# A one-core gated attention and expert block: causal mask as rows of the product, feed-forward in pairs, weights spread by a product

## What is computed

```python
xn = layernorm(x)
q, k, v = heads(xn @ Wq + bq), heads(xn @ Wk + bk), heads(xn @ Wv + bv)      # 16 heads of 8
y = softmax(where(causal, q @ k.T * D**-0.5, -inf)) @ v
y = y + softmax(qc @ kc.T * D**-0.5) @ vc     # qc = xn @ Wcq + bcq; kc, vc from the context
x = x + tanh(g_xattn) * (y @ Wp + bp)
xf = layernorm(x)
s = sigmoid(xf @ router.T); choice = s + router_bias           # 16 experts in 4 groups
# a group scores the sum of its best two choices; two groups stay; of their experts the best four
w = s[top4] / (sum(s[top4]) + 1e-20) * 2.5
x = x + tanh(g_ffn) * sum_e w[e] * (silu(xf @ wg[e].T) * (xf @ wu[e].T)) @ wd[e].T   # all 16 experts, width 64
```

## Time and profile before

| What | Value |
|---|---|
| median of 3 runs | 371.53 us (369.07 to 372.36) |
| profiled execution | 370.12 us |
| its span | 368.4 us |
| PE, DVE busy | 337.1 us (91%), 262.3 us (71%) |
| ACT, POOL busy | 199.4 us (54%), 199.3 us (54%) |
| DMA | 39.10 MB, mean 106 GB/s |

### The profile page before, as it was taken

How to read it: one execution, slowest core, us unless ns; L and a number is a source line. 1 busy time by engine, 2 the same in 40 slices (tenths; PEclk the granted TensorE clock), 3 DMA queues, 4 the chain that set the end, 5 groups by cost and what they waited for, 6 DMA issues and landing times.

```text
span 368.4 us, 8693 instructions
## 1 busy us (share of the span) xinstructions
PE 337.1 (91%) x3128; PEld 244.1 (66%) x3136; DVE 262.3 (71%) x710; ACT 199.4 (54%) x426; POOL 199.3 (54%) x296
## 2 busy tenths in 40 slices
PE   1778989999999999999999999999999999998665
PEld 0443554766776788777877877676877787766544
DVE  2228588567888878978787888777888856667752
ACT  2321256678757756665656646674666468633020
POOL 4945036608831796368824885449602842945305
PEclk9999999999999999999999999999999999999899
DMA  3254345664214653538143823183335003214060
GB/s 95 75 176 137 118 141 162 178 216 132 72 61 124 165 149 85 145 95 196 45 134 95 192 72 110 47 185 117 88 100 118 3 16 75 45 46 86 3 128 14
DMA packets 31322, 39.10 MB, mean 106 GB/s; under 512 B 2832, under 2 KB 28592, under 8 KB 28848
## 3 DMA queue, kind: packets, MB, share of 16 engines
q1 hardware_dynamic: 31280, 38.55, 38.7%
HBM read 30.89 MB, written 7.47 MB: 104 GB/s over the span
## 4 chain that ended last, share of the span: by engine, by line
PE 81%; DVE 7%; DMA 4%; ACT 3%; issue 2%; SPq 1%; POOL 1%; ACTq 0%; POOLq 0%
PE bank L743 14%; PE bank L721 13%; PE bank L708 9%; PE bank L812 7%; PE bank L813 6%; PE bank L821 6%; PE bank L705 5%; DMA k_stack<-part_scr 3%; PE bank L699 3%; PE bank L763 3%; PE bank L750 2%; PE bank L765 2%; PE bank L772 2%; PE bank L782 2%; PE bank L770 1%
## 5 line engine op out<-in xcount | busy, mean ns | idle before, releaser
L866 DVE TENSOR_REDUCE row_max<-bank 128x2 f32<-128x512 f32 (+1 forms) x224 | 149.2, 687 | 47.2 <-PE bank L708 25.7
L632 ACT ACTIVATE probs<-bank 128x512 f32<-128x512 f32 x224 | 127.9, 594 | 62.2 <-PE bank L721 49.0
L721 PE MATMUL bank<-q_stack,k_stack 73*128 73x256 bf16 (+1 forms) x512 | 80.9, 259 | 0.4 <-ACT probs L632 0.3
L547 POOL TENSOR_SCALAR_AFFINE_SELECT probs<-probs 128x256 f32<-128x256 f32 (+1 forms) x96 | 45.2, 483 | 40.1 <-ACT probs L632 39.2
L743 PE MATMUL bank<-probs,v_ext 128*32 128x256 f32 (+1 forms) x1024 | 61.1, 358 | 0.0
L560 POOL TENSOR_TENSOR f_h<-f_h,comb 128x256 f32<-128x256 f32 x64 | 45.3, 725 | 24.9 <-DMA comb<-c_scr 20.7
L708 PE MATMUL bank<-k_stack,q_stack 72*128 72x256 bf16 x256 | 50.7, 290 | 3.3 <-DMA k_stack<-part_scr 2.0
L721 PEld LDWEIGHTS bank<-q_stack,k_stack 73*128 73x128 bf16 x512 | 42.1, 98 | 16.8 <-issue 5.7
L812 PE MATMUL bank<-xn2T,w_pairs_sb 128*128 128x256 f32 x128 | 41.1, 403 | 3.4 <-DVE f_h L951 3.3
L743 PEld LDWEIGHTS bank<-probs,v_ext 128*32 128x32 f32 x1024 | 27.0, 109 | 22.5 <-issue 7.9
L944 DVE SCALAR_TENSOR_TENSOR f_gate<-f_tanh,bank 128x256 f32<-128x256 f32 x64 | 26.5, 413 | 19.9 <-ACT f_tanh L647 19.9
(11 more groups left out here) (103 smaller groups left out, 393.6 us busy)
## 6 DMA issues: line engine op xcount, KB each, us to landing
q_stack<-part_scr SPq DMA_DIRECT2D x48, 192.0 KB
k_stack<-part_scr SPq DMA_DIRECT2D x48, 192.0 KB
comb<-c_scr SPq DMA_DIRECT2D x16, 512.0 KB, 6.4
part_scr<-part SPq DMA_DIRECT2D x48, 128.0 KB, 2.0
x_in<-in_x SPq DMA_DIRECT2D x8, 128.0 KB, 2.9
w_pairs_sb<-in_w_pairs SPq DMA_DIRECT2D x1, 1024.0 KB, 7.7
out<-y_out SPq DMA_DIRECT2D x8, 128.0 KB, 1.9
ctx_in<-in_ctxT SPq DMA_DIRECT2D x8, 64.0 KB, 3.4
```

Of the source, the lines that this page charges most:

```text
L547: nc.gpsimd.affine_select(out=p, in_=p, compare_op=ALU.is_ge, fill=0.0, base=0, pattern=[[0, nh], [1, 128]], channel_multiplier=-1).then_i ...
L632: nc.scalar.activation(probs[:, seq % NP, :], exp_bank[s % 2][:, :], ACT.Exp).then_inc(exp_done, 1)
L721: last = pe.matmul(ps[:, n, :], k_stack[0:STACK + 1, b % SLOTS, kind, h, kt * 128:(kt + 1) * 128], q_stack[0:STACK + 1, b % SLOTS, kind, h ...
L866: nc.vector.tensor_reduce(row_max[:, kind, qt, h0:h0 + nh], max_bank[k % 2][:, :].rearrange("p (h k) -> p h k", h=nh), AX.X, ALU.max).then ...
```

## The change

**Causal rows.** The stacks of kind SELF get 48 more rows, 73 to 120. Of 128 tokens three share a row. A key has a factor in its own row only; a query has a large negative factor in the rows of all later keys and zero in those of earlier ones, and the three columns of a row are told apart by powers of two. The product over rows 0 to 120 is the masked score, in both passes, for the chunks' diagonal blocks; other blocks contract 72 or 73 rows as before. So a product of 256 queries over the diagonal becomes two of 128. The mask product and POOL's selections go. The rows are made once by POOL, placed in slot 0 by two DMAs and copied to slots 1 and 2 (`tri:0`, `tri:0:1`, `tri:0:2`); since row 72 lies among the rows now contracted in the first pass, a DMA zeroes it in `q_stack` with each load of a SELF stack.

**First cross stack in halves.** For sample 0 the cross stacks are loaded in halves of eight heads (`kh:0`, `qh:0`, `kh:0:1`, `qh:0:1`), all cross chunks are ordered by half, and the first shift is made and written for eight heads (`shift:0`), then for the rest (`shift:0:2`). Sample 0 is normalised on DVE (`xnv`), and so is the second layernorm of sample 7 (`xnv2`).

**Paired feed-forward.** Gates of two blocks fill one bank (`ga`), ups another (`up`); tanh, swish, the up product and POOL's product work on 512 columns, four of each a sample in place of eight. Each has one bank: the next `ga` waits for swish, the next `up` for the up product, the first `ga` of a sample for the `out` of the one before.

**Last weights by a product.** For sample 7 a 16 x 1024 matrix of ones and zeros, made by POOL in the unused tile `rest`, spreads the transposed weights over the partitions by products into four banks that the scores no longer need; ACT copies them to `comb`.

```diff
+ROW_TOKENS = 3
+ROWS = 48
+MASKED = STACK + 1 + ROWS
+AT = (2.0 ** 40, 2.0 ** -12, 2.0 ** -64)
+FROM = (2.0 ** -70, 2.0 ** -18, 2.0 ** 34)
+LATER = 2.0 ** 92
...
-S1_CHUNKS = [(CROSS, qt, 2 * g, 2, 256) for qt in range(NQ) for g in range(8)]
+S1_CHUNKS = [(CROSS, qt, H // 2 * half + 2 * g, 2, 256) for half in range(2) for qt in range(NQ) for g in range(4)]
...
-GU_USES = NB + 1
-ROUTE_STEPS = 18
+STACK_DMAS = (2 * PARTS, 2 * PARTS + 1)
+GP = NB // 2
+ROUTE_STEPS = 16
+ROUTE_WORDS = (0, 3, 6, 9, 12, 14, 16)
...
-        ident_b = sb("ident_b", [128, 128], BF16)
-        causal = sb("causal", [128, 4, 128], BF16)
+        tri_q, tri_k = (sb(n, [ROWS, 128 + ROWS * ROW_TOKENS], BF16) for n in ("tri_q", "tri_k"))
+        zero_row = sb("zero_row", [H, T], BF16)
...
+        expert_of = rest[0:E].rearrange("e k x -> e (k x)")
...
+            def place_masks(s):
+                if s == 0:
+                    sp.wait_ge(const_made, 3)
+                else:
+                    sp.wait_ge(tri_in[0], 32)
+                for st, tri in ((q_stack, tri_q), (k_stack, tri_k)):
+                    first = tri[:, 0:T].unsqueeze(1).broadcast_to([ROWS, H, T])
+                    src = first if s == 0 else st[SHIFT_ROW + 1:MASKED, 0, SELF]
+                    sp.dma_start(st[SHIFT_ROW + 1:MASKED, s, SELF], src).then_inc(tri_in[s], 16)
...
+                if kind == SELF and qk == 0:
+                    if b == 0:
+                        sp.wait_ge(const_step, 4)
+                    sp.dma_start(q_stack[SHIFT_ROW:SHIFT_ROW + 1, b % SLOTS, SELF], zero_row[:, :]).then_inc(stack_in[b % SLOTS][SELF], 16)
+            def load_first(qk, half):
+                sp.wait_ge(part_out[CROSS], 48)
+                heads = slice(half * H // 2, (half + 1) * H // 2)
+                for i in range(PARTS):
+                    src = scr[0, CROSS, qk, :, :, heads].rearrange("j d h x -> d j (h x)")
+                    if qk == 0:
+                        src = src[:, i].unsqueeze(1).broadcast_to([D, PARTS, H // 2 * T])
+                    sp.dma_start((q_stack, k_stack)[qk][i * BLOCK:(i + 1) * BLOCK, 0, CROSS, heads], src).then_inc(stack_in[0][CROSS] if half else first_heads_in, 16)
...
+                    heads = slice(H // 2 * (n // 2), H // 2 * (n // 2 + 1))
+                    sp.dma_start(q_stack[SHIFT_ROW:SHIFT_ROW + 1, 0, CROSS, heads], shiftT[heads, CROSS, :]).then_inc(shift_in[0][CROSS] if n else first_shift_in, 16)
...
+                at_q, at_k = (a[:, 128:].rearrange("p (r c) -> p r c", c=ROW_TOKENS) for a in (tri_q, tri_k))
+                for c in range(ROW_TOKENS):
+                    nc.gpsimd.memset(at_q[:, :, c:c + 1], -AT[c]).then_inc(const_step, 1)
+                    nc.gpsimd.memset(at_k[:, :, c:c + 1], FROM[c]).then_inc(const_step, 1)
+                pool.wait_ge(const_step, 4 + 2 * ROW_TOKENS)
+                earlier = dict(pattern=[[1, ROWS], [0, ROW_TOKENS]], channel_multiplier=-1)
+                nc.gpsimd.affine_select(out=at_k, in_=at_k, compare_op=ALU.is_equal, fill=0.0, base=0, **earlier).then_inc(tri_step, 1)
+                nc.gpsimd.affine_select(out=at_q, in_=at_q, compare_op=ALU.is_ge, fill=-LATER, base=0, **earlier).then_inc(tri_step, 1)
+                pool.wait_ge(tri_step, 2)
+                nc.gpsimd.affine_select(out=at_q, in_=at_q, compare_op=ALU.is_ge, fill=0.0, base=0,
+                                        pattern=[[-1, ROWS], [0, ROW_TOKENS]], channel_multiplier=1).then_inc(tri_step, 1)
+                pool.wait_ge(tri_step, 3)
+                for tri in (tri_q, tri_k):
+                    nc.gpsimd.tensor_copy(tri[:, 0:128], tri[:, 128:256]).then_inc(const_made, 1)
...
+            def mark_experts():
+                for kind in (CROSS, SELF):
+                    pool.wait_ge(split[kind], B * PARTS)
+                at = expert_of.rearrange("e (f u) -> e f u", u=I)
+                nc.gpsimd.memset(at, 1.0).then_inc(expert_step, 1)
+                pool.wait_ge(expert_step, 1)
+                nc.gpsimd.affine_select(out=at, in_=at, compare_op=ALU.is_equal, fill=0.0, base=0,
+                                        pattern=[[1, E], [0, I]], channel_multiplier=-1).then_inc(expert_step, 1)
             def combine(b, j):
-                pool.wait_ge(gu_free, b * GU_USES + j + 1)
-                if j == 0:
+                pool.wait_ge(ups_free, b * GP + j + 1)
+                if b == B - 1:
+                    pool.wait_ge(spread_done, j + 1)
+                elif j == 0:
                     pool.wait_ge(comb_in, b * 32 + 32)
-                at = f_h[:, j, :]
-                nc.gpsimd.tensor_tensor(at, at, comb[:, j, :], ALU.mult).then_inc(f_hc_done, 1)
+                at = f_h[:, 2 * j:2 * j + 2, :]
+                nc.gpsimd.tensor_tensor(at, at, comb[:, 2 * j:2 * j + 2, :], ALU.mult).then_inc(f_hc_done, 1)
...
+            def spread_out(b, j):
+                act.wait_ge(spread_ready, j + 1)
+                if j == 0:
+                    ge(act, f_hc_done, GP * b)
+                nc.scalar.activation(comb[:, 2 * j:2 * j + 2, :], spread_bank[j][:, :].rearrange("p (n x) -> p n x", n=2),
+                                     ACT.Copy).then_inc(spread_done, 1)
...
-                    pe.matmul(ps[:, :, keys - 128:keys], ident_b[:, :], causal[:, 0:nh, :], start=True, stop=False)
                 for n in range(nh):
-                    h = h0 + n
-                    q = q_stack[0:STACK, s, kind, h, qt * 128:(qt + 1) * 128]
+                    q, key = q_stack[:, s, kind, h0 + n, qt * 128:(qt + 1) * 128], k_stack[:, s, kind, h0 + n, :]
                     if kind == SELF:
-                        for kt in range(keys // 128):
-                            last = pe.matmul(ps[:, n, kt * 128:(kt + 1) * 128], q, k_stack[0:STACK, s, kind, h, kt * 128:(kt + 1) * 128],
-                                             start=False, stop=n == nh - 1 and kt == keys // 128 - 1)
+                        for kt in range(qt + 1):
+                            rows_used = MASKED if kt == qt else STACK
+                            last = pe.matmul(ps[:, n, kt * 128:(kt + 1) * 128], q[0:rows_used], key[0:rows_used, kt * 128:(kt + 1) * 128],
+                                             start=n == 0 and kt == 0, stop=n == nh - 1 and kt == qt)
...
+                    key, q = k_stack[:, b % SLOTS, kind, h, kt * 128:(kt + 1) * 128], q_stack[:, b % SLOTS, kind, h, :]
+                    if kind == SELF:
+                        for qt in range(kt, NQ):
+                            rows_used = MASKED if kt == qt else STACK + 1
+                            last = pe.matmul(ps[:, n, qt * 128 - q0:(qt + 1) * 128 - q0], key[0:rows_used], q[0:rows_used, qt * 128:(qt + 1) * 128],
+                                             start=n == 0 and qt == kt, stop=n == nh - 1 and qt == NQ - 1)
+                    else:
+                        last = pe.matmul(ps[:, n, :], key[0:STACK + 1], q[0:STACK + 1], start=n == 0, stop=n == nh - 1)
...
+            def hidden(b, j, bank_of, w):
+                for n in range(2):
+                    e0 = (2 * j + n) * 128
+                    last = pe.matmul(bank_of[:, n * T:(n + 1) * T], w[:, e0:e0 + 128], xn2T[:, :], start=True, stop=True)
+                return last
+            def gates_of(b, j):
                 if j == 0:
                     misc_evacuated(pe, "xn2T", b)
                     if b == 0:
                         pe.wait_ge(w_experts, 32)
-                use = b * GU_USES + j
-                ge(pe, gu_free, use - 1)
-                e0 = slice(j * 128, (j + 1) * 128)
-                pe.matmul(gu_bank[use % 2][:, 0:T], w_gate[:, e0], xn2T[:, :], start=True, stop=True)
-                pe.matmul(gu_bank[use % 2][:, T:2 * T], w_up[:, e0], xn2T[:, :], start=True, stop=True).then_inc(gu_ready, 1)
+                    ge(pe, out_made, b)
+                ge(pe, f_gate_done, b * GP + j)
+                hidden(b, j, gate_bank, w_gate).then_inc(gates_ready, 1)
+            def ups_of(b, j):
+                ge(pe, ups_free, b * GP + j)
+                hidden(b, j, up_bank, w_up).then_inc(ups_ready, 1)
...
+            def spread_weights(b, j):
+                if j == 0:
+                    misc_evacuated(pe, "combT", b)
+                    pe.wait_ge(expert_step, 2)
+                    pe.wait_ge(max_taken, B * NC1)
+                    pe.wait_ge(exp_done, B * NC2)
+                for n in range(2):
+                    last = pe.matmul(spread_bank[j][:, n * T:(n + 1) * T], expert_of[:, (2 * j + n) * 128:(2 * j + n + 1) * 128], combT[:, :],
+                                     start=True, stop=True)
+                last.then_inc(spread_ready, 1)
...
+                    last = nc.vector.scalar_tensor_tensor(out=r_score[:, :, :], in0=r_tanh[:, :, :], scalar=0.5,
+                                                          in1=spread(r_half[:, :].broadcast_to([128, NQ]), E), op0=ALU.mult, op1=ALU.add)
...
```

(17 more changed lines are left out.)

484 lines of the change are left out of this document (246 added, 238 removed).

## The result

| | before | after |
|---|---|---|
| median, beside each other | 370.32 us (4 runs) | 365.61 us (4 runs, 363.39 to 367.45) |
| profiled execution, span | 370.12, 368.4 | 365.4, 363.7 |

The ratio is 0.9864, 95% interval [0.9824, 0.9904]: faster by 1.4%, where 6.5% was forecast. 365.4 lies 19.0 us above the 346.4 of the sum. Stages are compared within traces; there is one trace for each kernel.

The account below looks back on a forecast made before the run. It took chains and DVE to pace the start, PE the long middle, one chain the end. 370.12 - 12.3 - 1.0 - 1.8 + 1.0 - 8.0 - 1.6 = 346.4, forecast 346 us (341 to 349, chance 0.62).

Parts of the forecast that it names:

- Mask products: PE-bound middle: removing 12 mask products a sample saves 1.76 us in each of seven samples, 12.3 us.
- rival A: Middle: hand-overs with a late DVE turn mask time into waiting, taking 9 of the 12.3 us, so 355; chance 0.12.
- Normalising on DVE: Start: normalising sample 0 on DVE instead of POOL makes all that hangs on it 1.0 us earlier.
- First exponential: Start: sample 0's first exponent product comes 2.8 us earlier, two thirds of it recovered idle time, 1.8 us.
- Single gate banks: Feed-forward: with one bank each, PE's gates wait for tanh and swish at times; charged 1.0 us.
- Routing: Sample 7's routing: two steps fewer and less slowing by POOL's products, less 0.4 given back; 1.6 us saved.
- the slow rows agree: Routing: slow steps fit the skill's two-input rule, by which rewriting frees nothing; the sum would be 1.6 us higher.
- End after routing: From sample 7's routing to the output sum: 18.1 us becomes 10.1, a gain of 8.0 us.
- Rival B: Mask-row copies delay the start up to 6 us, or sample 6's weights stall the end; 350 to 352, chance 0.14.

Follow-up runs that it names:

- m2: Kernel before with the causal rows alone, mask copies of slot 1 issued at `load:3`; 369.73 us, ratio 0.9933.
- e1: Changed kernel with POOL's memset of v_ext moved behind the second rstd; 363.2 us, ratio 0.9782.
- e3: e1 with the start's loads and stores in order of need and slot 1's mask copies issued at `load:3`; 364.66 us, ratio 0.9832.
- c1: m2 with eight unread products in sample 0 where mask products stood; 367.88 us, ratio 0.9942.
- m1: Kernel before with the causal rows alone, mask copies of slot 1 issued behind sample 1's key stack; 372.06 us, ratio 1.0005.
- c2: e1 with nine unread products in PE's gaps between 36 and 47 us; 360.35 us, ratio 0.9725.
- d1: e1 with the last sample's weights sent through DRAM again instead of spread by a product; 369.13 us, ratio 0.9895.
- t1: Kernel before with only the last weights spread by a product, feed-forward still in eight blocks; 377.65 us, ratio 1.0181.
- e2: e1 with the start's loads and stores in order of need and slot 1's mask copies behind sample 1's stacks; 368.14 us, ratio 0.9917.
- h1: e1 with POOL's product of a pair split into two of 256 columns; 363.68 us, ratio 0.9791.
- g1: e1 with the first routing steps of sample 1 placed between sample 3's reductions on DVE; 364.3 us, ratio 0.9774.
- z1: c2 with g1's routing order; 362.08 us, ratio 0.9740.

## Why the prediction was wrong

The direction held and the price of nearly every step was off. By its own terms:

**Mask products, -12.3.** This is the step that failed: "seven samples count", because PE is busy 39.94 of 40 us in the middle. Causal rows alone gave 2.5 us in the median and 3.3 in the middle of the trace. The work fell by 8.8 to 10 (the 128-column products, at 58 ns and not 55, cost 2.6; I had an upper bound of 1.3 us and took zero), and 5.3 us of it turned into waiting, 3.5 of them waits for shift rows and stacks. This is rival A's mechanism, with DMA beside DVE: in m2 the new waits are for DMA, in after the longest are for DVE. A full PE says what bounds now, not how far the next bound is. Here it was within 1 us a sample.

**Normalising on DVE, -1.0.** The first maximum came 2.8 us later: 3 us for the memset beside the step, shown by e1. Of the constants made first on POOL I had counted nothing; they cost 0.8 (rstd at 5.43 against 4.66 before).

**First exponential, -1.8.** It was forecast 2.8 us earlier and came 3.1 later. With memset and stores mended it comes 2.6 earlier (44.9), so the reading of the two orders was right. Worth in time: nothing that the ratios show (e3 0.9832, e1 0.9782). Its 3 us at sample 1 were more than half gone by sample 3, one wait for a stack among the causes, and the rest went with a half-speed stretch of that one trace.

**Half speed in the start, no term.** The maxima of sample 0 were costed at DVE's pace, with the mask products there as free to lose. Without them full speed comes at 57.6 (m2), with products that nobody reads in their place at 44.8 (c1). Only one of them (43.08) lies ahead of the rise at 43.7, and in m1, which has none, the clock rose at 43.6 too and fell again from 47.0 to 57.2: what they did, as far as the traces show it, is keep the speed. In the first 30 us behind its first maximum product, PE gets through 16.5 us of work (at full-speed prices) before and 13.5 after; 1.6 of the 3.0 are sample 0's mask products themselves. In m2 the lost speed and the lost work balance: sample 1's first maximum comes 24.2 us behind sample 0's, for 24.1 before. In the changed order more hangs on it: 30.3 us in e1, 27.1 with fillers (c2), whose last exponential ends 3.1 us earlier.

**Single gate banks, +1.0.** No cost is seen: PE's idle time ahead of gates and ups is 1.5 us in after and 3.4 before. No run took the banks alone.

**Routing, -1.6.** It was -3.0 (7.45 to 4.48): no step is held any more, as POOL's products end before it begins. The five steps that were held gave 2.7 of it (3.6 to 0.9), two steps fewer the rest. The timing gave the 2.7, not the new forms, as the Trainium skill's rule on two inputs ("SBUF — State Buffer", "Who interferes with whom") says; the trace agrees: steps of 0.17 to 0.19 us here took up to 1.20 in the middle. My "the slow rows agree" holds for four of the five; the first (0.80) is a tensor_scalar with one input, of which that rule says nothing.

**End after routing, -8.0.** It was -3.6 (18.14 to 14.56). The term that was mis-sized: 0.43 us for a pair of gates. A row's x2 counts instructions, and one float32 product of 256 columns is two. So ten groups of gates, ups and spreading, four instructions each, take 0.96 to 1.06 us each and 9.9 together (347.32 to 357.23), the down products 3.7, and PE is the bound from routing to output, not the loop over tanh and swish. That the product is worth having is shown by d1 (4.2 us longer by the ratio; 5.3 in its trace, some 2 of it clock) for the paired kernel; in the kernel before the same product made it 1.8% slower (t1, with 13.7 us of half speed). Another 2.5 us are gained between the last exponential and the routing: 3.1 us of feed-forward products stand ahead of the last exponential that stood behind it.

**Rival B** named the copies ahead of the first loads. In after they delay nothing that bounds: with them moved behind, in e3, the first maximum comes at the same 28.4 us as in e1. Placed near 61 to 63 us (m1, e2) they made a wait of 3 to 4 us, and half speed around it.

The pieces add up: +2.8 to the first maximum; from there to the last exponential -9.4 of work gone, +3.1 of work moved ahead, and the rest, +7.9, of waiting and half speed, so +1.6; behind it -2.5, -3.0 and -3.6. Together -4.7, as measured. Of the 7.9, 3.0 are the slow start and 4.8 come from losses of over 0.6 us: after has four (79.4, 143.3, 262.2, 323.9; 5.7 together), before one of 0.9; the one at 143 has its cause shown (h1, g1), but taking it away shortened nothing (z1, level with c2 again by sample 6), so its share of the time is not 2.2 us. The one at 323.9 is the wait for sample 6's routing on DVE. What is open: how much of the remaining stalls is the written order, which another order might avoid.

## What to carry over

Before pricing removed work on a full engine at its whole length, find what the next wait would be: the loads of each sample, and how early they land. Work taken from TensorE where another engine paces it can be no gain: without sample 0's mask products the way to sample 1's first maximum was as long as with them (24.2 us for 24.1), and nine useless products in such a stretch, with the memset moved, made the kernel with the lowest time (360.35 us, 0.9725 [0.9684, 0.9765]; without them 363.2 us and 0.9782, whose interval overlaps). Count the products of a float32 group by the code, not by the x of a row.

## What the runs showed of the hardware

- A memset on GpSimd that reads nothing held a tensor_scalar on VectorE for 3 us (3.57 against 0.60).
- A small VectorE step with two inputs ends no sooner than the GpSimd product that is running, and the next step is held by the next product: 1.20 us beside a product of 1.28, 1.18 beside one of 1.16, 0.65 beside 0.73, and 0.17 to 0.19 alone.
- TensorE was busy for 14.40 of 15 us (after) and 15.65 of 17 (e2) while it went at half speed for nearly all of them; in c2, with small products in gaps of 0.25 to 0.36 us, full speed came 14 us earlier than in e1. Around an idle time of 3.2 to 3.3 us there were 3.4 us of half speed (before), 13.7 (t1) or 17.1 (e2).
- Products of 128 columns start 58 to 59 ns apart in both kernels with causal rows, whether they contract 72 or 121 rows, and 55 in the kernel before. Why those with 72 rows are slower too was not tried.
